# Two-layer local-attention and FFN kernel: 64x64 score products without their masked corners, and one output product for the FFN's last 42 channels

## The reference

```
h = shift_token(x);  q, k, v = split(h @ wqkv)          # 8 heads of 64
q, k = rotary_xpos(l2norm(q) * qs, l2norm(k) * ksc)
bq, bk, bv = windows of 128 queries; keys and values of the window and the one before
sim = where((i < j) | (i > j + 128) | (j == -1), -max, bq @ bk.T)   # i query, j key
x = x + (softmax(sim) @ bv) @ wo
h = layernorm(shift_token(x)) * lg + lb
a, g = split(h @ w1 + b1)                                # 2 x 682 channels
x = x + (a * gelu(g)) @ w2 + b2
```

## Time and profile before

| | |
|---|---|
| median of 3 runs | 1422.95 us (1420.28 to 1424.81) |
| profiled execution | 1424.29 us, its span 1422.5 us |
| granted TensorE clock, mean | 0.991 |
| busy: PE, DVE, ACT, POOL | 97%, 68%, 62%, 54% of the span |
| causal attention | to about 200 us |
| one steady step | 74.15 us |

### The profile page before, as it was taken

How to read it: one execution, slowest core, us unless ns; L and a number is a source line. 1 busy time by engine, 2 the same in 40 slices (tenths; PEclk the granted TensorE clock), 3 DMA queues, 4 the chain that set the end, 5 groups by cost and what they waited for, 6 DMA issues and landing times.

```text
span 1422.5 us, 24115 instructions
## 1 busy us (share of the span) xinstructions
PE 1374.8 (97%) x7740; PEld 1050.5 (74%) x7740; DVE 963.8 (68%) x2671; ACT 878.1 (62%) x2223; POOL 762.1 (54%) x522
## 2 busy tenths in 40 slices
PE   6999997999999999999999999999999999999988
PEld 5878775777777777777777777786777777777756
DVE  6877765767676666666667777676767676766657
ACT  4556656575747575747475766666565757575763
POOL 2425765564647373738373747464655646473710
PEclk9999999999999999999999999999999999999998
DMA  7111100000000000000001010000000000000046
GB/s 220 38 51 60 55 30 1 1 1 0 0 0 0 0 0 0 0 0 0 0 1 60 14 47 1 1 0 0 0 0 0 0 0 0 0 0 0 0 145 210
DMA packets 35243, 33.33 MB, mean 23 GB/s; under 512 B 8364, under 2 KB 32896, under 8 KB 35200
## 3 DMA queue, kind: packets, MB, share of 16 engines
q1 hardware_dynamic: 35200, 32.79, 7.3%
HBM read 24.39 MB, written 8.39 MB: 23 GB/s over the span
## 4 chain that ended last, share of the span: by engine, by line
PE 78%; ACT 11%; DVE 5%; issue 4%; POOL 1%; DMA 0%; ACTq 0%; SPq 0%; DVEq 0%; POOLq 0%
PE l_psF L1399 9%; PE l_psP L842 9%; PE l_ring L842 9%; PE l_ring L1399 8%; PE l_ring L1469 7%; ACT l_att L1073 7%; PE l_psP L1453 6%; PE l_psF L1487 6%; PE l_psS L1410 5%; PE l_psS L1422 4%; PE l_ring L653 3%; PE l_psF L1439 2%; PE l_psS L671 1%; PE l_psP L688 1%; ACT L1163 1%
## 5 line engine op out<-in xcount | busy, mean ns | idle before, releaser
L955 POOL TENSOR_TENSOR l_att<-l_att 128x1024 f32<-128x1024 f32 x64 | 153.1, 2403 | 315.7 <-DVE l_att L880 315.7
L1007 POOL TENSOR_TENSOR l_att<-l_att,l_rinv 128x1024 f32<-128x1024 f32 x64 | 126.4, 1975 | 70.7 <-DVE l_rinv L1243 70.4
L1053 ACT ACTIVATE l_att<-l_psP 128x384 f32<-128x384 f32 (+1 forms) x128 | 70.3, 549 | 120.7 <-PE l_psP L1453 120.4
L1248 DVE COPY l_att<-l_psP 128x384 f32<-128x384 f32 (+1 forms) x128 | 78.9, 617 | 86.7 <-PE l_psP L1453 82.5
L1453 PE MATMUL l_psP<-ident,l_att 128*128 128x128 f32 x896 | 124.5, 279 | 2.0 <-DVE l_att L1248 1.5
L1453 PEld LDWEIGHTS l_psP<-ident,l_att 128*128 128x128 f32 x896 | 98.6, 141 | 32.4 <-issue 28.2
L962 POOL TENSOR_TENSOR l_att<-l_att,l_rn 128x1024 f32<-128x1024 f32 x64 | 120.8, 1910 | 0.7 <-ACT l_rn L861 0.5
L1073 ACT ACTIVATE l_att<-l_psF,l_nb 128x256 f32<-128x256 f32 x256 | 118.1, 483 | 2.1 <-DVE l_nb L1236 2.1
L971 POOL TENSOR_TENSOR l_u_lo<-l_att,l_u_hi 128x512 fp32r<-128x512 f32 x75 | 95.7, 1288 | 39.1 <-ACT l_u_hi L1048 39.0
L1469 PE MATMUL l_ring<-l_att 128*64 128x256 f32 (+1 forms) x1024 | 112.5, 362 | 2.0 <-ACT l_att L1053 1.4
L1236 DVE CUSTOM_DVE_ANT_0 l_psF<-l_psF,w_mask 128x256 f32<-128x256 f32 x256 | 101.1, 456 | 16.3 <-issue 16.3
(11 more groups left out here) (209 smaller groups left out, 4037.2 us busy)
## 6 DMA issues: line engine op xcount, KB each, us to landing
a_tables<-in_x SPq DMA_DIRECT2D x8, 512.0 KB, 4.3
scratch_s<-a_o SPq DMA_DIRECT2D x8, 512.0 KB, 3.2
l_att<-in_x SPq DMA_DIRECT2D x8, 512.0 KB, 8.8
l_att<-scratch_s SPq DMA_DIRECT2D x8, 512.0 KB, 9.0
out_dram<-l_att SPq DMA_DIRECT2D x7, 512.0 KB, 7.8
aw_stage<-in_wqkv SPq DMA_DIRECT2D x2, 768.0 KB, 5.9
l_att<-in_wqkv SPq DMA_DIRECT2D x2, 768.0 KB, 5.4
w_w_raw<-in_w SPq DMA_DIRECT2D x2, 640.0 KB
```

The costliest lines, as they stand in the source:

```text
L955: pool.tensor_tensor(rot[:, t, :], rot[:, t, :], t2[t % 2], ALU.add).then_inc(S["added"], 1)
L1007: pool.tensor_tensor(pr, pr, along(inv, 2 * P), ALU.mult).then_inc(S["p_done"], 1)
```

## The change

Scores: each product of 128 queries becomes two of 64 queries, in the column halves of the array, over the 192 keys that any of the 64 can see (128 for the first query tile). The corners that are left out keep what the PSUM place held before, and `least_of` adds the mask to it as before. In steps with an FFN the first query tile of unit 1 stays whole. The waits of `scores` move to `score_operands`, which such steps call ahead of the last product or transpose before the scores (`ahead`).

The last 42 channels: the rows of the sixth tile are filled with three copies, so that one product sums all three parts. Rows 0 to 41 are the channels, 42 to 51 and 52 to 61 hold channels 32 to 41 again, 64 to 95 and 96 to 127 channels 0 to 31 again. Weights, b1 and w2 are loaded that way (thirteen loads more in the causal attention's step 0 with the mask `less`, eight of them for b1 and four for w2; four more for each layer's w1); ACT copies U_hi once more into rows 96 to 127; DVE makes the low parts in two instructions. The diff, cut to its core:

```diff
+BAND = P // 2
+AGAIN = HREM - 32
...
     def load_w1(self, sp, layer, stage):
...
+            for r in range(2):
+                c1 = c + HREM + r * AGAIN
+                sp.dma_start(stage[:, :, c1:c1 + AGAIN], w1[:, :, (s + 1) * HID - AGAIN:(s + 1) * HID]).then_inc(self.S["w1_in"], 16)
...
     def load_w2(self, sp, layer):
...
-        sp.dma_start(self.w2_raw[0:HREM, HFULL, :], self.io["w2"][layer, HFULL * P:HID]).then_inc(self.S["w2_in"], 16)
+        for p0, first, n in ((0, 0, HREM), (HREM, 32, AGAIN), (HREM + AGAIN, 32, AGAIN), (64, 0, 32), (96, 0, 32)):
+            row = HFULL * P + first
+            sp.dma_start(self.w2_raw[p0:p0 + n, HFULL, :], self.io["w2"][layer, row:row + n]).then_inc(self.S["w2_in"], 16)
...
+        sp.dma_start(self.less[:, :], io["fless"]).then_inc(small, 16)
...
+                for r in range(2):
+                    p0 = s * GATE0 + HREM + r * AGAIN
+                    sp.dma_start(self.b1col[p0:p0 + AGAIN, l, 2 * HFULL:W1T], rest[32:HREM], allow_slow_non_contiguous=True).then_inc(small, 16)
...
+    def end_w2(self, dve, layer):
+
+        end = (slice(0, P), HFULL)
+        dve.wait_ge(self.S["small"], self.SMALL)
+        dve.wait_ge(self.S["w2_hi"], layer + 1)
+        dve.scalar_tensor_tensor(out=self.w2_hi[end], in0=self.w2_hi[end].bitcast(F32), scalar=self.less[:, 1:2], in1=self.w2_raw[end],
+                                 op0=ALU.mult, op1=ALU.add).then_inc(self.S["w2_end"], 1)
...
         def u_high(i, j, attn):
-            rows = P if j < HFULL else HREM
+            rows = P if j < HFULL else GATE0
             ge(act, S["u_done"], HT * (i - 1) + j + 1)
             act.activation(U_hi[0:rows, j, :], gate_of(j, attn)[0:rows, :], ACT.Copy).then_inc(S["u_hi"], 1)
+            if j == HFULL:
+                act.activation(U_hi[96:P, j, :], gate_of(j, attn)[0:32, :], ACT.Copy).then_inc(S["u_again"], 1)
...
         def u_low(i, j, attn):
-            rows = P if j < HFULL else HREM
+            u = gate_of(j, attn)
             ge(dve, S["u_hi"], HT * (i - 1) + j + 1)
-            dve.tensor_tensor(U_lo[0:rows, j, :], gate_of(j, attn)[0:rows, :], U_hi[0:rows, j, :].bitcast(F32), ALU.subtract).then_inc(low_done(0, j)[0], 1)
+            if j < HFULL:
+                dve.tensor_tensor(U_lo[:, j, :], u, U_hi[:, j, :].bitcast(F32), ALU.subtract).then_inc(S["u_lo"], 1)
+            else:
+                dve.scalar_tensor_tensor(out=U_hi[32:GATE0, j, :], in0=U_hi[32:GATE0, j, :].bitcast(F32), scalar=W.less[32:GATE0, 0:1],
+                                         in1=u[32:GATE0, :], op0=ALU.mult, op1=ALU.add)
+                dve.tensor_tensor(U_hi[64:96, j, :], u[0:32, :], U_hi[0:32, j, :].bitcast(F32), ALU.subtract).then_inc(S["u_lo_last"], 1)
...
-        def down(i, c, tiles):
+        def down(i, c, tiles, l, ahead=None):
 
             for k in tiles:
                 if c == 0:
                     ge(pe, *low_done(i - 1, k))
-                for m, (w, u) in enumerate(((W.w2_hi, U_hi), (W.w2_hi, U_lo), (W.w2_lo, U_hi))):
-                    last = pe.matmul(down_of[c], w[:, k, c * P:(c + 1) * P], u[:, k, :], start=(k == 0 and m == 0), stop=(k == HT - 1 and m == 2))
+                    if k == HFULL:
+                        ge(pe, S["u_again"], i)
+                        pe.wait_ge(WS["w2_end"], l + 1)
+                for m, (w, u) in enumerate(((W.w2_hi, U_hi), (W.w2_hi, U_lo), (W.w2_lo, U_hi))[:1 if k == HFULL else 3]):
+                    if ahead is not None and k == tiles[-1] and m == 2:
+                        score_operands(i, ahead)
+                    last = pe.matmul(down_of[c], w[:, k, c * P:(c + 1) * P], u[:, k, :], start=(k == 0 and m == 0), stop=(k == HFULL))
...
-        def scores(i, u, tiles=0):
+        def score_operands(i, u, tiles=TT):
+
+            if u < 2:
+                ge(pe, S["qT_sb"], TT * i + tiles)
+                ge(pe, S["kT_sb"], TT * i + tiles)
+            else:
+                ge(pe, S["exp_done"], UNITS * i + u - 1)
+
+        def scores(i, u, whole=0):
+
...
             for tt in range(2):
                 t = half * 2 + tt
-                c0 = 0 if t else P
                 for par in range(2):
                     rows = slice(par * DH, (par + 1) * DH)
-                    last = pe.matmul(ps[:, par * 512 + tt * 2 * P + c0:par * 512 + (tt + 1) * 2 * P], QT[rows, pair, t * P:(t + 1) * P],
-                                     KT[rows, pair, max(t - 1, 0) * P:(t + 1) * P], start=True, stop=True, skip_group_check=True)
+                    c = par * 512 + tt * 2 * P - (t - 1) * P
+                    for part in range(1 if tt < whole else 2):
+                        n = P if tt < whole else BAND
+                        q = t * P + part * BAND
+                        k0, k1 = (q - P, q + n) if t else (0, P)
+                        last = pe.matmul(ps[part * BAND:part * BAND + n, c + k0:c + k1], QT[rows, pair, q:q + n], KT[rows, pair, k0:k1],
+                                         start=True, stop=True, skip_group_check=True)
...
-        def p_transposes(i, u):
+        def p_transposes(i, u, ahead=None):
...
+                        if ahead is not None and par and tt and own:
+                            score_operands(i, ahead)
...
             if attn and ffn:
                 scores(i, 0)
                 ge(pe, S["u_done"], HT * (i - 1) + HFULL)
+                scores(i, 1, 1)
...
-                down(i, 0, range(0, 4))
+                down(i, 0, range(0, 4), lf, ahead=2 if attn else None)
...
                     if ffn and u in (2, 4):
-                        down(i, 0, range(3 + u // 2, 4 + u // 2))
+                        down(i, 0, range(3 + u // 2, 4 + u // 2), lf, ahead=u + 1 if u == 2 else None)
                     if u >= 5 and u % 2:
                         values(i, (u - 5) // 2, ffn)
                     if u >= 3:
-                        p_transposes(i, u - 3)
+                        p_transposes(i, u - 3, u + 1 if ffn and u + 1 < UNITS else None)
```

More of the change, by code:

```diff
@@ L94, in __init__ @@
         self.b2col = sb("b2", [P, LAYERS, KD])
+        self.less = sb("less", [P, 2])
         self.cosT = sb("cos", [P, LAYERS, TT, 2, DH])
@@ L173, in low_wo @@
         dve.tensor_tensor(self.wo_lo[:, :, :], self.wo_raw[:, :, :], self.wo_hi[:, :, :].bitcast(F32), ALU.subtract).then_inc(self.S["wo_lo"], 1)
-    def w2_parts(self, layer):
-        return ((slice(0, P), slice(0, HT)),) if layer == 0 else ((slice(0, P), slice(0, HFULL)), (slice(0, HREM), slice(HFULL, HT)))
     def high_w2(self, act, layer):
[L181 to L184, removed]
+        act.wait_ge(self.S["w2_in"], 96 * (layer + 1))
+        act.activation(self.w2_hi[:, :, :], self.w2_raw[:, :, :], ACT.Copy).then_inc(self.S["w2_hi"], 1)
     def low_w2(self, dve, layer):
+        full = slice(0, HFULL)
         dve.wait_ge(self.S["w2_hi"], layer + 1)
-        for r, k in self.w2_parts(layer):
-            last = dve.tensor_tensor(self.w2_lo[r, k, :], self.w2_raw[r, k, :], self.w2_hi[r, k, :].bitcast(F32), ALU.subtract)
-        last.then_inc(self.S["w2_lo"], 1)
+        dve.tensor_tensor(self.w2_lo[:, full, :], self.w2_raw[:, full, :], self.w2_hi[:, full, :].bitcast(F32), ALU.subtract).then_inc(self.S["w2_lo"], 1)
+    def end_w2(self, dve, layer):
[4 more added lines that the diff above has]
+                                 op0=ALU.mult, op1=ALU.add).then_inc(self.S["w2_end"], 1)
 class Shared:
@@ L968, in u_low @@
         def u_low(i, j, attn):
-            rows = P if j < HFULL else HREM
             ge(pool, S["u_hi"], HT * (i - 1) + j + 1)
-            pool.tensor_tensor(U_lo[0:rows, j, :], gate_of(j, attn)[0:rows, :], U_hi[0:rows, j, :].bitcast(F32), ALU.subtract).then_inc(low_done(0, j)[0], 1)
+            pool.tensor_tensor(U_lo[:, j, :], gate_of(j, attn), U_hi[:, j, :].bitcast(F32), ALU.subtract).then_inc(S["u_lo"], 1)
         def step(i, la, lf, last=False):
@@ L1349, in step @@
                 dve.wait_ge(C.a_dma, 16 * (B + 1))
-                dve.wait_ge(S["zeros"], 1)
-                for half in (U_hi, U_lo):
-                    dve.tensor_copy(half[:, HFULL, :], C.zero[:, :].broadcast_to([P, N]))
+                W.end_w2(dve, 0)
             if last:
@@ L1383, in variance, with hidden @@
             pe.matmul(psF[:, N:2 * N], ones[:, :], sqF[:, 0, :], start=True, stop=True).then_inc(S["var_ps"], 1)
-        def hidden(i, j, attn, parts=("hi", "lo")):
+        def hidden(i, j, attn, parts=("hi", "lo"), ahead=None):
             u = i - 1
@@ L1397, in hidden @@
                     for n, (k, w, a) in enumerate(terms):
+                        if ahead is not None and n == 3 * KD - 1:
+                            score_operands(i, ahead)
                         if (a is flo) == (wanted == "lo"):
@@ L1507, in step @@
                 ge(pe, S["x_attn"], KD * i)
-                down(i, 0, range(HT))
-                down(i, 1, range(0, 3))
+                down(i, 0, range(HT), lf)
+                down(i, 1, range(0, 3), lf)
```

(12 more changed lines are left out.)

43 lines of the change are left out of this document (21 added, 22 removed).

## The result

The changed kernel takes 1483.8 us (median of 4 runs, 1482.8 to 1484.6), the kernel before 1423.9 on the same chip: ratio 1.0429 (1.0416 to 1.0443), so 60 us slower. I had said 1430 in a range of 1412 to 1442: slower was right, its size and most of its cause were not.

A forecast was written before the change was run, and what follows sets the result against it. It took the softmax stretch to hang on a chain of waits through ACT's exponentials, despite PE's 97% busy. Start +4.7, first step -.9, fifteen steady steps +3.2, last step 0 gave +7 on 1422.95: 1430 us, range 1412 to 1442.

The forecast's parts named there:

- DVE's u_low, "+.65, in time": Softmax stretch: u_low becomes two DVE instructions, +.65 us, with unit 3's minima still in time for its exponentials.
- The clock, "I leave it there": Steady step: granted clock stays 1.00 (2.4 GHz), since PE's new waits are under 1 us.
- Moved waits and 64x64 products, +.68 together with the copy on ACT: Softmax stretch: held evacuations and ACT's .52 us second copy make it .68 us longer a step.
- Dense stretch, -.47: Behind the softmax stretch: two fewer output products of the last tile save .47 us a step.
- First step, -.9: Attention-only step: four score groups on its path give -.9 us (0 to -1.4).
- The start, +4.7: Kernel start: thirteen more loads delay the third batch's load and stall DVE by 4.7 us (bounds +2.5 to +5.8).
- Last step, 0: Last step: u_low adds .65, two products fewer save .47, DVE's final additions follow anyway: 0 (-.5 to +.3).
- quadrants in turn: Rival, score products: column halves of one row half don't overlap, +1.2 us a step, 1452 us; chance .13.
- Evacuations not held: Rival, softmax stretch: ACT's path grows by the copy alone, -.87 us a step, 1414 us; chance .17.
- PE-bound: Rival, steady steps: PE's whole saving counts, (1.2 + .93) us a step, 1395 us; chance .08.

The follow-up runs named there:

- e5: The last-42-channels part alone on the kernel before, with GpSimd's normalisation of unit 1 held until DVE has made the last U_hi rows; 1437.8 us (1.0103).
- e10: e5 with the second copy into U_hi made by GpSimd, adding a tile of zeros, instead of by ACT; 1432.4 us (1.0075).
- e9: The changed kernel with six unused products on PE between the first half's last output product and unit 1's transposes; 1464.0 us (1.0296).
- e1: The changed kernel with GpSimd's normalisation of unit 1 held until DVE has made the last rows of U_hi; 1441.9 us (1.0135).
- e4: The kernel before with only the score part of the change, 64x64 products and moved waits; 1428.4 us (1.0041).
- e8: e1 with the three output products of tile 4, second column half, after the transposes of unit 6 instead of before; 1433.0 us (1.0066).
- e2: The changed kernel with the score waits back at the scores, on a one-column product ahead of each group; 1487.8 us (1.0463).
- e3: The kernel before with only the last-42-channels part of the change, score products and their waits as before; 1482.9 us (1.0431).
- e11: e10 with e8's edit and the loads of layer 1's small tables and w2 issued right behind the seventh batch's load; 1420.3 us (.9985).
- e12: e11 with 64x64 score products in the attention-only first step besides; 1420.8 us (.9987).

## Why the prediction was wrong

By its own steps:

- *DVE's u_low, "+.65, in time": the step that failed.* Two things were wrong with it. First, the price. I took .65 for each instruction from a row in which DVE goes first; behind GpSimd it is 2.48, and 1.74 of that is waiting. Second, the question "in time for whom". I followed DVE to unit 3's minima and asked only for their exponentials. Behind the minima stands DVE's copy of unit 0's transposes, and for that copy wait unit 1's. Even at its own price the extra .77 (two rows, .74 + .68, for one of .65) came out on the path: .74 in e5 and e10, where I had put nothing.
- *The clock, "I leave it there".* The argument was that PE's new waits are under 1 us. The new wait was 1.74, and in thirteen of fifteen steps the clock fell behind it and cost 1.5 us more. A wrong duration on DVE thus became a wrong clock on PE; e9 prices the second at 20 us.
- *Moved waits and 64x64 products, +.68 together with the copy on ACT.* The mechanism is there: .88 and .70 us of PE's time before the transposes named. The size was wrong in its parts. Moved waits with 64x64 products cost .35 (e1 less e5) or .32 (e4); the copy on ACT cost nothing at the values of pair 1 (e10), where the walk had .52.
- *Dense stretch, -.47: wrong.* PE does save .47 there, but the next transposes wait for DVE's copy of unit 6 and start no earlier: .51 of wait. The trace of before showed them on the edge (1.62 us from unit 6's transposes to unit 7's, .03 of it idle; after: 1.62 again). A stretch in which PE never idles need not be bound by PE. e8 fills the gap and gets the half microsecond.
- *First step, -.9: borne out for the products.* It became 1.8 shorter, 75.1 for 76.9. In e1 and e5 the clock was low equally long there (0.83 in the first 20 us, 1.00 behind), and they take 75.1 with 64x64 products and 76.0 without: -.9. The other -.9 no product explains: e5 has the products of before. In before the clock fell in two places of this step (0.91 in the first 20 us and 0.91 in the next), in e5 in one.
- *The start, +4.7: right, in part by luck.* The first projection starts at 192.5 instead of 187.6, +4.9. SP had issued the thirteen loads faster than I took (the third batch's load goes out at 32.06, not 34.3), but the load took 7.8 us, and the statistics began at 39.9 instead of near 41. From 3.8 us at the statistics 4.9 came at the projection. In the seven other runs with the same loads in this place (e1, e2, e3, e5, e8, e9, e10) it starts at 189.9 to 192.3, +2.3 to +4.7; with the loads moved to a free place (e11) at 186.8.
- *Last step, 0:* +.2.

The sum from the traces: 4.9 - 1.8 at the start and in the first step; in the steady steps 15 x 1.48 = 22 for the wait behind GpSimd, 13 x 1.5 = 20 for the clock, 15 x .74 = 11 for DVE's second instruction, 15 x .35 = 5 for the moved waits; the dense stretch 0, the end .2. That makes 61, and the two spans differ by 60.0. Some of these terms were sized with the runs, so that the sum comes out is no further proof of them.

Of the rivals, *quadrants in turn* is refuted: four 64x64 products run together (unit rows of .78 and .88 us, starts 7 ns apart), as the Trainium skill (TensorEngine Tiling, Key Properties) lets them. *Evacuations not held* and *PE-bound* fall with the waits of .88 and .70. None of the four named GpSimd, although gave it two thirds of the stretch: I had looked at who waits for GpSimd's results, not at what it reads.

## What to carry to other kernels

When an instruction is added or changed, look at what the other engines do beside it in that very place, not only at its row elsewhere: on DVE, an instruction with two inputs in SBUF beside a GpSimd instruction can cost the rest of GpSimd's. Follow each delay through the engine's whole queue and ask for every reader behind it; the copy that was missed here stood one unit further on. Price a wait on PE twice, once as time and once as the clock that may fall behind it.

## What the runs showed that was not expected

- DVE and GpSimd exclude each other here in both directions: 2.48 instead of .74 on DVE, 2.45 instead of 1.89 on GpSimd, and which it is changes from step to step of one execution (twelve and three).
- Behind a wait of 1.74 us on PE the clock fell to its lower level for some 3.3 us in thirteen of fifteen steps, in twelve and eleven with the same wait in e2 and e3; what spares a step stays open. After 1.06 us at the same place (e10) it fell in none. Idle products in the wait kept it at 1.00 and made the kernel 20 us faster.
- Taking .47 us of products out of a stretch in which PE was never idle gave nothing, and moving others into the gap gave .5.
- The projection's products started 228 ns apart instead of 233 in the three kernels with the tile of zeros (e10, e11, e12). That is some 5 us of 1420, more than what separates e11 from the kernel before; the cause stays open.
